# Two fused transformer layers on one core: a new SyncE order for set-up and a new table of times for block 0's attention

## What is computed

```python
def _L0_cond_ref(x, pos_ids, time_emb, ln1_w, ln1_tw, ln2_w, ln2_tw, Wq, Wk, Wv, Wo, Wg, Wu, Wd):
    h = ada_rms(x, time_emb, ln1_w, ln1_tw)      # n * (w * (1 + t @ tw.T))
    q, k, v = h @ Wq.T, h @ Wk.T, h @ Wv.T       # 8 query heads, 1 key/value head, 64 wide
    q, k = apply_rope(q, pos_ids), apply_rope(k, pos_ids)
    attn = softmax(q @ k.T / 8)
    x = x + (attn @ v) @ Wo.T
    h = ada_rms(x, time_emb, ln2_w, ln2_tw)
    return x + silu(h @ Wg.T) * (h @ Wu.T) @ Wd.T
def _L1_cond_ref(...):
    gamma1, gamma2, scale1, scale2, shift1, shift2 = silu(cond) @ Wada.T + bada   # one row per sequence
    x = x + attn(_ln(x) * (scale1 + 1) + shift1) * gamma1     # 16 heads, cosine attention
    x = x + mlp(_ln(x) * (scale2 + 1) + shift2) * gamma2      # GELU, 512 -> 2048 -> 512
```

## Time and profile before

| | us |
|---|---|
| median of 3 runs | 2596.08 |
| lowest, highest | 2592.76, 2596.55 |
| the profiled execution | 2595.27 |
| its span | 2593.3 |
| PE busy in the span | 2506.8 (97%) |
| DVE, ACT, POOL busy | 1388.8, 961.7, 1062.5 |

### The profile page before, as it was taken

One profiled execution on the slowest core, in us unless ns is written; L12 is line 12 of the kernel. 1 busy time (PEld: TensorE's weight loads), 2 busy tenths in 40 slices (PEclk: granted clock), 3 DMA queues, 4 the chain that ended last, 5 costly groups with the idle time before them and its releaser, 6 DMA issues.

```text
span 2593.3 us, 47329 instructions
## 1 busy us (share of the span) xinstructions
PE 2506.8 (97%) x18448; PEld 1259.8 (49%) x18448; DVE 1388.8 (54%) x2150; ACT 961.7 (37%) x1560; POOL 1062.5 (41%) x1007
## 2 busy tenths in 40 slices
PE   6589999999999999999999999999999999999998
PEld 5344444454444544444454445454545455454543
DVE  6464343443434424344486485766757585766741
ACT  4343232232322323223343462635445262635442
POOL 2233132232222322223353464655556464665532
PEclk8799999999999999999999999999999999999999
DMA  6430100001000010100322412121121212111110
GB/s 205 131 122 5 51 3 29 28 5 51 3 32 24 5 51 3 40 17 7 126 83 75 134 30 71 34 59 42 53 65 30 83 28 73 38 55 46 51 41 29
DMA packets 119126, 133.21 MB, mean 51 GB/s; under 512 B 51855, under 2 KB 62351, under 8 KB 118933
## 3 DMA queue, kind: packets, MB, share of 16 engines
q1 hardware_dynamic: 118932, 130.26, 16.7%
HBM read 75.83 MB, written 18.74 MB: 36 GB/s over the span
## 4 chain that ended last, share of the span: by engine, by line
PE 83%; DVE 5%; POOL 4%; issue 4%; ACT 3%; DMA 1%; SPq 1%; POOLq 0%; DVEq 0%; ACTq 0%
PE ps_m L1555 46%; PE ps_abef L1555 18%; PE ps_d L1555 2%; PE ps_c L1555 2%; PE ps_abef L1762 2%; PE ps_abef L1755 2%; PE ps_abef L1757 2%; PE ps_abef L1791 1%; PE ps_d L1741 1%; PE ps_c L1607 1%; POOL inner L904 1%; POOL scratch L932 1%; PE ps_abef L1799 1%; PE ps_abef L1780 1%; POOL scratch L936 1%
## 5 line engine op out<-in xcount | busy, mean ns | idle before, releaser
L1555 PE MATMUL ps_m<-h_mlp,weights 128*128 128x512 f16 x3264 | 747.6, 380 | 17.1 <-ACT scratch L1168 10.1
L1555 PE MATMUL ps_m<-weights,inner 128*128 128x512 f16 x3072 | 695.5, 380 | 2.1 <-DVE scratch L1388 2.1
L1555 PEld LDWEIGHTS ps_m<-h_mlp,weights 128*128 128x128 f16 x3264 | 312.9, 98 | 379.8 <-ACT scratch L1168 16.6
L904 POOL TENSOR_TENSOR inner<-scratch,inner 128x512 f16<-128x512 f32 x256 | 310.3, 1212 | 399.6 <-ACT inner L1089 399.5
L1555 PEld LDWEIGHTS ps_m<-weights,inner 128*128 128x128 f16 x3072 | 296.5, 98 | 337.4 <-issue 6.2
L1555 PE MATMUL ps_abef<-h_mlp,weights 128*128 128x512 f16 x1344 | 310.9, 379 | 0.0
L1089 ACT CAST inner<-scratch 128x512 f16<-128x512 f32 x256 | 157.0, 613 | 155.6 <-DVE scratch L1388 84.3
L1555 PEld LDWEIGHTS ps_abef<-h_mlp,weights 128*128 128x128 f16 x1344 | 127.1, 98 | 144.8 <-issue 4.2
L882 POOL TENSOR_TENSOR h_mlp<-scratch,h_mlp 128x512 f16<-128x512 f32 x64 | 73.9, 1155 | 193.5 <-ACT h_mlp L1044 193.5
L944 POOL TENSOR_TENSOR scratch<-scratch 128x512 f32<-128x512 f32 x64 | 72.5, 1133 | 159.4 <-DVE scratch L1442 159.4
L1044 ACT CAST h_mlp<-scratch 128x512 f16<-128x512 f32 x64 | 39.5, 618 | 263.7 <-POOL scratch L944 142.1
(11 more groups left out here) (170 smaller groups left out, 3729.1 us busy)
## 6 DMA issues: line engine op xcount, KB each, us to landing
x_mlp<-x_attn SPq DMA_DIRECT2D x64, 256.0 KB, 2.3
scratch<-scratch SPq DMA_DIRECT2D x128, 128.0 KB
weights<-gamma SPq DMA_DIRECT2D x128, 128.0 KB, 3.0
...
inner<-wada_t SPq DMA_DIRECT2D x4, 1024.0 KB, 6.8
```

The costliest lines, as they stand in the source:

```text
L904: nc.gpsimd.tensor_tensor(inner[:, 1, j, :], src[:, j % 2, :], inner[:, 0, j, :], ALU.subtract).then_inc(L.m_lo, 1)
L1555: ins = nc.tensor.matmul(o, left(a, k), right(b, k), start=(first and n == 0), stop=(last and n == len(order) - 1), skip_group_check=True)
```

## The change

It alters the order of block 0's attention with the set-up, the layout of the rotary tables, and where some DMAs stand in SyncE's queue. No compute instruction is added or taken away.

```diff
+def hands_late(plan, second_norms):
+    last = max([at for at, s, t in plan if s == "spread"] + second_norms[:-1]) + 1.5
+    times = [last] * (TILES - 1) + [max(last, second_norms[-1]) + 4.0]
+    moved = [(at + wait, s, t) for t, at in enumerate(times) for s, wait in (("hand", 0.0), ("next", 3.0))]
+    return [m for m in plan if m[1] != "hand"] + moved
...
-FIRST0_STARTS, FIRST0_SECOND = [9.4, 24.4, 39.4, 53.7], [47.2, 60.9, 74.4, 108.2]
+FIRST0_STARTS, FIRST0_SECOND = [10.3, 25.0, 39.8, 54.6], [46.3, 61.2, 76.7, 184.5]
 SETUP0 = [
-    (0, "consts", 0), (1.7, "ang", 0), (4.0, "ang", 1), (6.8, "sin", 0), (6.9, "load", "ada4"), (7.3, "load", "ada5"),
+    (0, "ada_out", 0), (0, "load", "ada4"), (1.6, "load", "gate0"), (3.1, "consts", 0), (5.3, "ang", 0),
...
-FIRST0 = [m[1:] for m in sorted(attention_plan(CHAIN0F, NORM0F, FIRST0_STARTS, FIRST0_SECOND) + SETUP0, key=lambda m: m[0])]
+FIRST0 = hands_late(attention_plan(CHAIN0F, NORM0F, FIRST0_STARTS, FIRST0_SECOND), FIRST0_SECOND) + SETUP0
+FIRST0 = [m[1:] for m in sorted(FIRST0, key=lambda m: m[0])]
...
-        rope_dram = nc.dram_tensor("rope_tables", (P, NBLK * TILES, 2, 32), F32, kind="Internal").ap()
+        rope_dram = nc.dram_tensor("rope_tables", (P, 2, NBLK * TILES, 32), F32, kind="Internal").ap()
...
-        rope = carve(TILES * 64).rearrange("p (t s f) -> p t s f", t=TILES, s=2)
+        rope = carve(TILES * 64).rearrange("p (s t f) -> p t s f", t=TILES, s=2)
...
-                sp.wait_ge(L.hand, handed)
+                if L is L1 or not first_block(it):
+                    sp.wait_ge(L.hand, handed)
...
             def rope_of(it):
-                sp.dma_start(rope.rearrange("p t s f -> p (t s f)"), ...)
+                src = rope_dram.rearrange("p s (n t) f -> p s n (t f)", n=NBLK)[:, :, bass.ds(it, 1)]
+                sp.dma_start(rope.rearrange("p t s f -> p s t f"), src.rearrange("p s o (t f) -> p s (o t) f", t=TILES)).then_inc(L0.rope_in, 16)
...
                     sp.dma_start(b_fc1_t, b_fc1).then_inc(s_l1c, 16)
+                if piece == "rows":
                     for copy in range(2):
                         for n, row in ((0, q_bias), (2, b_proj), (3, b_fc2)):
...
-                        sp.dma_start(rope_dram[:, rest, n, :],
+                        sp.dma_start(rope_dram[:, n, rest, :],
...
                 if stage == "hand":
-                    move_on(L0, NORMS0F, x, 0, a, True)
+                    hand_over(L0, NORMS0F, 0, a)
+                if stage == "next":
+                    sp.wait_ge(L0.hand, 16 * max(a + 1, TILES - 1))
+                    next_x(L0, NORMS0F, x, 0, a)
```

More of the change, by code:

```diff
@@ L132 @@
     ("turn_p", 29.9), ("c_lo", 29.9), ("key_major", 30.3), ("c_hi", 30.9), ("mix", 32.5), ("out", 35.3), ("add", 37.9)]
-NORM0F = list(zip([s for s, _ in NORM0], [0.0, 0.8, 1.1, 2.9, 3.4, 5.9, 5.9]))
+NORM0F = list(zip([s for s, _ in NORM0], [0.0, 0.2, -1.3, 3.9, 2.9, 4.7, 5.1]))
 CHAIN0F = [(s + "1", at) for s, at in NORM0F] + [
-    ("proj", 7.1), ("rot", 8.5), ("qk_lo", 8.7), ("qk_hi", 12.3), ("feature_major", 15.1), ("spread", 15.8),
-    ("shift", 16.4), ("turn", 16.8), ("scores", 17.2), ("exp", 18.0), ("soft", 19.0), ("p_hi", 21.1), ("p_lo", 21.9),
-    ("turn_p", 22.3), ("c_lo", 24.2), ("key_major", 25.6), ("mix", 25.7), ("c_hi", 25.8), ("out", 26.4), ("add", 26.7)]
+    ("rot", 6.0), ("proj", 8.4), ("qk_lo", 8.6), ("qk_hi", 10.0), ("spread", 11.9), ("feature_major", 17.1),
+    ("turn", 17.3), ("p_lo", 17.3), ("scores", 17.4), ("shift", 17.4), ("soft", 17.8), ("exp", 19.3), ("p_hi", 19.9),
+    ("key_major", 23.8), ("c_hi", 23.9), ("turn_p", 24.1), ("c_lo", 24.4), ("mix", 24.8), ("add", 26.6), ("out", 29.1)]
 PE_COST0 = {"turn_x1": 0.45, "turn_x2": 0.45, "proj": 3.3, "turn": 0.6, "scores": 0.5, "turn_p": 0.5, "mix": 0.9, "out": 2.6}
@@ new lines @@
+    (0, "ada_out", 0), (0, "load", "ada4"), (1.6, "load", "gate0"), (3.1, "consts", 0), (5.3, "ang", 0),
+    (5.9, "ang", 1), (7.3, "load", "up0"), (9.2, "sin", 0), (9.2, "load", "ada5"), (9.7, "rope", 0),
+    (11.5, "cut", "qkv"), (11.6, "ada", 0), (13.3, "cut", "qkv_v"), (14.8, "load", "ada2"), (15.3, "ang", 2),
+    (15.7, "sin", 1), (18.6, "cut", "wo"), (19.0, "rope", 1), (20.2, "ada", 1), (22.5, "rows", 0),
+    (24.8, "load", "ada6"), (25.2, "sin", 2), (28.8, "ang", 3), (29.0, "ada_out", 1), (31.9, "ada", 4),
@@ new lines @@
+    (32.8, "rope", 2), (40.6, "sin", 3), (42.9, "rope", 3), (43.7, "rope_out", 0), (44.2, "cut", "gate0"),
+    (44.4, "ada", 5), (47.0, "load", "ada3"), (47.4, "load", "ada7"), (52.0, "load", "up1"), (54.3, "bias", 0),
+    (56.6, "ada", 6), (57.0, "ada_out", 6), (59.3, "ada", 7), (59.8, "cut", "up0"), (62.5, "bias", 1),
+    (64.5, "ada_out", 4), (64.7, "load", "gate1"), (65.0, "load", "up2"), (68.8, "ada_out", 3), (72.8, "cut", "gate1"),
+    (74.6, "bias", 2), (76.1, "ada", 2), (76.3, "ada", 3), (78.6, "ada_out", 2), (79.7, "load", "gate2"),
@@ L155 @@
+    (92.1, "ada_out", 5), (95.2, "load", "up3"), (108.3, "cut", "up1"), (109.0, "load", "gate3"),
+    (109.1, "ada_out", 7)]
 SETUP_START0 = [
[3 rows of a table removed]
[3 rows of a table added]
 SETUP_LAST0 = [(85.0 + 5.0 * n, "cut1", n) for n in range(8)] + [(86.0 + 5.0 * n, "load1", n + 2) for n in range(6)]
@@ L187 @@
                                                      for n in range(4)])
-SETUP_STEPS = ("consts", "bias", "load", "load1", "cut", "cut1", "ada", "ada_out", "ang", "sin", "rope", "rope_out")
+SETUP_STEPS = ("consts", "rows", "bias", "load", "load1", "cut", "cut1", "ada", "ada_out", "ang", "sin", "rope", "rope_out")
 MLP0 = SETUP_STEPS + ("gate", "up", "down", "gamma_m", "tanh", "gated", "m32", "m_hi", "m_lo", "y", "store")
@@ L678, in rope_of @@
             def rope_of(it):
-                sp.dma_start(rope.rearrange("p t s f -> p (t s f)"), rope_dram.rearrange("p (n t) s f -> p n t s f", n=NBLK)[:, bass.ds(it, 1)].rearrange("p o t s f -> p (o t s f)")).then_inc(L0.rope_in, 16)
+                src = rope_dram.rearrange("p s (n t) f -> p s n (t f)", n=NBLK)[:, :, bass.ds(it, 1)]
+                sp.dma_start(rope.rearrange("p t s f -> p s t f"), src.rearrange("p s o (t f) -> p s (o t) f", t=TILES)).then_inc(L0.rope_in, 16)
             def next_tables(L, dram, norms, it):
```

## The result

The changed kernel takes 2580.87 us as the median of 5 runs (2577.09 to 2582.70), against 2596.08 before: a ratio of 0.9938, 95% interval 0.9926 to 0.9951, so 15.2 us less. The forecast was 2582.5 us in a range of 2575.5 to 2588.5.

What follows compares the result with a forecast made beforehand. PE's products bound everything after the first `gate` product; before it PE idled 53 us, mostly around DMA waits. Walking block 0's checkpoints moved that product 13.6 us: 2595.27 − 13.6 = 2581.7, plus 0.8 for the median, 2582.5 us; range 2575.5 to 2588.5.

Steps and rivals of the forecast that it cites:

- The bound: PE's products set the time after the first `gate` product at 137.76 us; the change's worth is moving that point, −13.6.
- Up to `proj:1`: Block 0's start: `scale1:0` and `rope:0` fill DVE's wait, freeing 0.35 us ahead of `proj:0` and 0.25 ahead of `turn:0`: −0.6.
- `proj:2`: `lo1:2` behind a slowed `p_lo:1` on POOL; PE stands 3.4 us, last eight products take 2.2 at lower clock: +3.8.
- `mix:1` and `out:1`: `mix:1` starts at 70.5 (−5.9), `out:1` takes 4.5 us at the lower clock, `turn:2` starts at 80.7 (−7.65).
- rival (a): Clock does not fall at `proj:2`, or `ada:4` and `proj:1` run at full clock: 3.3 and up to 2.7 us more gain; chance 0.3.
- `proj:3` to `ada:2`: `turn:2` to end of `proj:3` 10.1 us (−6.95); `out:2` waits for `rot:3`, ends 98.45 (−14.1); 2.9 us to `ada:2`.
- `turn_p:3`: Gate1 lands 5.4 us after issue, delaying `exp:3` by 1.6 us; `turn_p:3` starts at 110.0: −12.5, 1.7 us given back.
- `mix:3` and `out:3`: `spread` of tile 3 lands just ahead of `key_major:3`; `mix:3` starts at 111.6, `out:3` ends at 115.7: −13.1.
- rival (b): More gain given back: lower clock around `mix:2`, late x of block 1, `START0` stall; 2584 to 2587 us; chance 0.2.
- The last norm: From the end of `out:3` to the MLP's start: 8.45 us instead of 8.9, so the MLP starts at 124.15: −13.6.
- (c): SyncE reaches `spread` of tile 1 only where before; both long waits stay, gain shrinks to within 5 us; chance 0.04.
- (d): Slower: gate1's load gates `exp:3`; decides from a landing 24 us after issue, 27 us gives 2604; chance 0.03.

Runs made afterwards that it cites:

- b_spread_first: The kernel before with only the table stores (short runs) moved behind `spread` of tile 1: 2588.93 us, ratio 0.9972.
- b_queue_spread: The kernel before with long-run stores behind spread:1, hand-overs behind spread:3, and loads of up1, ada6, gate2 moved behind spread:1 or spread:2: 2577.41 us, ratio 0.9921.
- a_again: The changed kernel once more, unedited, on the chip of batch 3: 2581.35 us, ratio 0.9946 to the kernel before.
- the three queue edits: The kernel before with long-run table layout, stores behind `spread` of tile 1, hand-overs and block 1's x loads behind `spread` of tile 3: 2585.95 us, ratio 0.9961.

## Why the prediction was right, point by point

**The bound.** Right. The gain is the move of the first `gate` product; from there to the end the 14 profiles took 2455.0 to 2458.6 us, and the changed kernel lies inside that with 2456.29. This scatter of 3.6 us is larger than some of the differences between the kernels above. `START0`'s new numbers, the bias rows, the table load with more runs and the late x loads cost nothing to be seen.

**Up to `proj:1`: −0.6 forecast, −3.8 measured.** This term was mis-sized, in part by the order and in part by what one profile can't tell. 0.83 us are the landing of the first weight (PE starts at 9.68 instead of 10.51; in the seven other profiles of the new order it lies between 8.91 and 10.48). The order gave 1.1 us where 0.35 + 0.25 were forecast: from PE's first product to `proj:0` 9.39 us instead of 9.99, from the end of `proj:0` to `turn:0` 6.22 instead of 6.70, and the other seven profiles of the new order show both within 0.1 us. The remaining 1.9 us are shorter products, `proj:0` 4.79 us instead of 6.23 and `proj:1` 4.30 instead of 4.81, and lie within the scatter: `proj:0` took 4.79 to 6.23 us over the 14 profiles, with 4.79 in b_spread_first, of the old order, too. Inside `proj:0` the products' pace doubles at some point, sooner in the one profile than in the other. The granted clock doesn't show it; it reads 1.00 in both. The changed kernel, then the one before:

```profile
20.00:22.00 2.00, 2.00 (x9) 1.02 (x8) 1.86 (x5) 0.00 (x0) 0.34 (x1) 1.00 1.05 388
22.00:24.00 2.00, 2.00 (x17) 1.28 (x16) 1.86 (x6) 0.15 (x1) 0.00 (x0) 1.00 1.06 407
...
24.00:26.00 2.00, 2.00 (x9) 1.03 (x8) 1.71 (x5) 1.03 (x1) 0.00 (x0) 1.00 0.08 9
26.00:28.00 2.00, 2.00 (x17) 1.67 (x16) 1.24 (x4) 0.88 (x1) 0.00 (x0) 1.00 0.63 84
```

From PE's first product to the end of `proj:1`, the six profiles with the old order of this part took 36.7 to 38.2 us, mean 37.5; the eight with the new one 35.2 to 37.0, mean 35.9.

**`proj:2`: right in mechanism and size.** `lo1:2` behind a `p_lo:1` that ran under the cut, a wait of 3.23 us (3.4 forecast), the last eight products at half clock in 2.31 us (2.2). Taking out the lead, it cost 4.5 us against 4.4. The Trainium skill (SBUF — State Buffer, "SBUF: two separate sides") has the engine that starts first hold the pair for its whole instruction. The runs agree: the cut that started 0.21 us ahead kept its 2.28 us and POOL took 3.08. In b_queue_spread POOL started at 65.37 and kept 1.15, and the cut from 65.41 took 3.26.

**`mix:1` and `out:1`: rival (a)'s price came, not its condition.** 10.2 us were forecast from `mix:1` to `turn:2`, 7.46 measured. The clock did fall at `proj:2`, but was back soon (granted 0.50 as the mean of 64 to 66 us, 0.94 of 66 to 68), so `out:1` took 2.75 us instead of 4.5 and the two small steps before it 0.9 us less. Rival (a) had named 2.75 us for `out:1`, but with a clock that doesn't fall and 1.1 us for the last products of `proj:2`, which took 2.31. What failed in the walk is the step that kept the clock down until `out:1`. I had taken its old length over from rows that followed an idle time of 11.20 us.

**`proj:3` to `ada:2`: right.** 10.3 us to the end of `proj:3` (10.1 forecast), then 7.3 to the end of `out:2` (7.65), which waits for `rot:3`, then 2.95 to `ada:2` (2.9).

**`turn_p:3`: right in mechanism, 1.2 us short.** Gate1 landed 6.43 us after its issue and not 5.4, and ACT stood 3.38 us for it.

**`mix:3` and `out:3`: 1.5 us short.** `mix:3` waited for `key_major:3`, not for its spread, as forecast; but the wait of 2.74 us before `turn_p:3` was followed by half clock, and `out:3` took 3.67 us. This is rival (b) in another place. **The last norm** took 7.5 us instead of 8.45.

The misses, −3.2 and −2.7 against +1.2, +1.5 and −0.9, leave 4.1 us at `gate`. So the forecast is as close as it is partly by luck: terms off by up to 3.2 us cancelled in part. In the medians 1.6 us remain of the 4.1, and 0.1 against the batch of a_again. The range's upper end should have been 2588.2 by its own terms (2587.2 and 1), not 2588.5.

**Rivals (c) and (d)** did not come. The bias rows held SyncE for less than the free time, and gate1's landing was far from 24 us.

**What I had not seen:** that the three queue edits would give two thirds or three quarters only, since in the old order both `spread` also stand behind a load that waits for PE. The forecast didn't need it, as it walked the new order; whoever copied the three edits alone would have got 3.5 to 5 us less.
